# First attention: scores and searches in 64-row tiles, two heads side by side in two banks

## The reference, cut to what matters

```
qkv = x @ w_qkv.T + b_qkv
q, k, v = jnp.split(qkv, 3, axis=-1)            # 16 heads of 8 columns each
q, k = _apply_rope(q, cos, sin), _apply_rope(k, cos, sin)
scores = jnp.einsum('bhsd,bhtd->bhst', q, k) / jnp.sqrt(jnp.float32(hd))
scores = jnp.where(causal[None, None, :, :], scores, -jnp.inf)
attn = jax.nn.softmax(scores, axis=-1)
out = jnp.einsum('bhst,bhtd->bhsd', attn, v)
return out @ w_out.T + b_out
```

## Time and profile before

| | us |
|---|---|
| median of three runs | 3714.76 |
| the profiled execution, its own time | 3713.15 |
| its span (first to last instruction) | 3711.4 |
| PE busy | 3239.8 (87%) |
| DVE busy | 2656.9 (72%) |
| ACT busy | 2004.8 (54%) |
| POOL busy | 588.2 (16%) |
| first attention: first to last exponential (L952) | 345.0 to 972.0 |

### The profile page before, as it was taken

How to read it: one execution, slowest core, us unless ns; L and a number is a source line. 1 busy time by engine, 2 the same in 40 slices (tenths; PEclk the granted TensorE clock), 3 DMA queues, 4 the chain that set the end, 5 groups by cost and what they waited for, 6 DMA issues and landing times. The chain is left out here.

```text
span 3711.4 us, 44165 instructions
## 1 busy us (share of the span) xinstructions
PE 3239.8 (87%) x14402; PEld 1960.8 (53%) x14402; DVE 2656.9 (72%) x6064; ACT 2004.8 (54%) x3427; POOL 588.2 (16%) x484
## 2 busy tenths in 40 slices
PE   4999999999899998779988777778799998589998
PEld 3775343443377764236544333334477776357776
DVE  5566778777355587777766888886777777777776
ACT  2444656555444445444435655543377775157776
POOL 0000000000000000000002544430023332013332
PEclk9999999999999999889999889889999999789999
DMA  2000101010000131003331000002411110011111
GB/s 78 1 24 21 39 24 36 19 44 10 22 10 1 59 97 51 1 31 97 101 105 59 1 0 1 1 17 84 135 59 46 42 31 23 0 41 35 38 47 49
DMA packets 89647, 146.27 MB, mean 39 GB/s; under 512 B 13085, under 2 KB 25565, under 8 KB 89289
## 3 DMA queue, kind: packets, MB, share of 16 engines
q1 hardware_dynamic: 89416, 143.43, 12.5%
HBM read 134.02 MB, written 9.34 MB: 39 GB/s over the span
## 5 line engine op out<-in xcount | busy, mean ns | idle before, releaser
L358 POOL TENSOR_TENSOR norm_rstd<-norm_rstd,minus_half 128x4 f32<-128x4 f32 x144 | 174.3, 1211 | 2210.7 <-DVE norm_rstd L349 2208.2
L952 ACT ACTIVATE main_tiles<-banks 128x512 f32<-128x512 f32 (+3 forms) x768 | 356.9, 490 | 246.3 <-PE banks L940 166.3
L2189 ACT ACTIVATE main_tiles_r<-banks,feature_cols 128x512 fp32r<-128x512 f32 x512 | 353.2, 690 | 190.4 <-PE banks L228 168.5
L821 DVE TENSOR_REDUCE gate_scratch<-banks 128x1 f32<-128x512 f32 (+3 forms) x608 | 367.1, 655 | 122.4 <-PE banks L771 94.7
L2197 DVE TENSOR_TENSOR main_tiles_r<-main_tiles,main_tiles_r 128x512 fp32r<-128x512 f32 x512 | 383.4, 764 | 69.9 <-ACT main_tiles L2190 68.4
L226 PE MATMUL banks<-normed_pairs,moe_weights 128*128 128x512 f32 x800 | 409.2, 512 | 18.4 <-ACT main_tiles L2190 7.1
L2190 ACT ACTIVATE main_tiles<-banks,feature_cols 128x512 f32<-128x512 f32 x512 | 350.2, 684 | 0.0
L227 PE MATMUL banks<-normed_pairs,moe_weights 128*128 128x512 f32 x800 | 318.2, 398 | 0.0
L228 PE MATMUL banks<-normed_pairs,moe_weights 128*128 128x512 f32 x800 | 317.8, 397 | 0.0
L2234 POOL TENSOR_TENSOR normed<-normed,main_tiles 128x512 f32<-128x512 f32 x128 | 217.7, 1701 | 538.7 <-DVE main_tiles L2223 538.7
L226 PE MATMUL banks<-main_tiles_r,moe_weights 128*128 128x512 f32 x640 | 266.5, 416 | 28.3 <-DVE main_tiles_r L2197 26.4
(11 more groups left out here) (333 smaller groups left out, 6788.3 us busy)
## 6 DMA issues: line engine op xcount, KB each, us to landing
main_tiles<-gates_d SPq DMA_DIRECT2D x400, 256.0 KB, 3.3
weight_staging<-in_w SPq DMA_DIRECT2D x33, 256.0 KB, 3.7
parts_d<-bf_parts SPq DMA_DIRECT2D x48, 128.0 KB, 1.8
q_stacks<-parts_d SPq DMA_DIRECT2D x192, 32.0 KB
k_stacks<-parts_d SPq DMA_DIRECT2D x192, 32.0 KB
x_res<-in_x_t SPq DMA_DIRECT2D x8, 256.0 KB, 3.4
out_x<-x_res SPq DMA_DIRECT2D x8, 256.0 KB, 3.7
rope<-in_rope SPq DMA_DIRECT2D x1, 1024.0 KB
```

Of the source, the lines that this page charges most:

```text
L821: eng.tensor_reduce(o, bank[:, 0:per * (k1 - k0)].rearrange("p (n c) -> p n c", n=per), AX.X, ALU.max).then_inc(s.ring_free)
L952: eng.activation(weight_tile(e)[:, 0:C - q0], psum[:, 4 + e % 2, 0:C - q0], ACT.Exp, scale=HD ** -0.5).then_inc(s.at_exp)
L2189: eng.activation(pair_3(j)[0], psum[:, 2 + j % 2, :], ACT.Relu, bias=bias)
```

## The change

1. Each score or search matmul reads 64 rows only (`q_of`, `k_of`) and names a tile position, row 0 for an even head and row 64 for an odd one. Heads 2j and 2j+1 are issued one behind the other, to two different banks.
2. A mask is added by `add_mask`: since a 64-row tile sees only half of the identity's rows, there are two matmuls for a head, one from each half of the rows; the half that lies in the other 64 rows comes from a copy with the halves exchanged (`matb_swapped`). One of the two has 128 columns, the other 64. So four small matmuls stand for a pair of heads, where there were two.
3. Scores go through three banks (4, 5, 6), in pairs: a pair (e, e+1) waits for exponential e-2. The row sums use bank 7 alone (before 6 and 7), so that the first one of each half waits for the copy of the half before; it is planned 4.4 behind its head instead of 2.6.
4. The search has 40 items for a group (before 38), each of one parity of heads: for the first 128 queries two items of two heads (256 columns) in place of one of four heads. Items are issued in pairs; a pair (n, n+1) waits until item n-2 was reduced, and DVE starts on the pair when both are there.
5. Planned times: a group every 31.0, a head every 0.62, a search item every 0.7.
6. At the start four more DMAs (ahead of x), one more DVE copy, and the wait for constants counts nine loads (144).
7. The waits of the second feed-forward block and of the first scores follow the banks.

```diff
+    matb_swapped = at("const_mats_bf_swapped", [P, 3 * P], BF16)
...
-    raw = main[:, 21, :]
+    raw, raw_swapped = main[:, 21, :], main[:, 20, :]
+    def add_mask(eng, o, side, mask):
+        for half in range(2):
+            m = (matb if half == side else matb_swapped)[64 * side:64 * side + 64, :]
+            c0, c1 = (64 * half, TILE) if mask == 1 else (0, 64 * half + 64)
+            z = eng.matmul(o[:, c0:c1], m[:, 0:P], m[:, mask * P + c0:mask * P + c1], start=False, stop=half == 1,
+                           tile_position=(64 * side, 0))
+        return z
...
+        for half in range(2):
+            to, of = slice(64 * half, 64 * half + 64), slice(64 - 64 * half, 128 - 64 * half)
+            eng.dma_start(raw_swapped[to, 0:P], mats[of, 0:P]).then_inc(s.const_in, 16)
+            eng.dma_start(raw_swapped[to, P:3 * P], mats[of, MATS["mask_st"]:MATS["mask_st"] + 2 * P]).then_inc(s.const_in, 16)
...
-        eng.wait_ge(s.const_in, 80)
+        eng.wait_ge(s.const_in, 144)
...
+        eng.tensor_copy(matb_swapped[:, :], raw_swapped[:, 0:3 * P])
...
-    GROUP_US = 42.0
+    GROUP_US = 31.0
...
-    HEAD_US = 0.83
+    HEAD_US = 0.62
+    ITEM_US = 0.7
...
-    for i in range(4):
-        per = (4, 2, 1, 1)[i]
-        SEARCH += [(i, h0, per, 0, (i + 1) * TILE) for h0 in range(0, 4, per)]
-    for i in range(4, 8):
-        per = (4, 2, 1, 1)[i - 4]
-        SEARCH += [(i, h, 1, 0, C) for h in range(4)]
-        SEARCH += [(i, h0, per, C, (i + 1) * TILE) for h0 in range(0, 4, per)]
+    for i in range(8):
+        per, k0 = (2, 2, 1, 1)[i % 4], C * (i // 4)
+        if i >= 4:
+            SEARCH += [(i, side, side + 2 * j, 1, 0, C) for j in range(2) for side in range(2)]
+        SEARCH += [(i, side, side + 2 * j, per, k0, (i + 1) * TILE) for j in range(0, 2, per) for side in range(2)]
...
-        return qs_t[:, g % 3, h // 2, j0:j1]
+        return qs_t[64 * (h % 2):64 * (h % 2) + 64, g % 3, h // 2, j0:j1]
...
-        return ks_t[:, g % 3, h, j0:j1]
+        return ks_t[64 * (h % 2):64 * (h % 2) + 64, g % 3, h, j0:j1]
...
+                if m % 2:
+                    continue
...
+                if n >= 2:
+                    eng.wait_ge(s.ring_free, n - 1)
+                i, _, h0, per, k0, k1 = SEARCH[m]
+                diag, width = k1 == (i + 1) * TILE, k1 - k0
+                for j in range(per):
+                    for side in range(2):
+                        o, h = ring_bank(n + side)[:, j * width:(j + 1) * width], h0 + 2 * j + side
+                        z = eng.matmul(o, q_of(g, h, i * TILE, (i + 1) * TILE), k_of(g, h, k0, k1), start=True,
+                                       stop=not diag, tile_position=(64 * side, 0))
+                        if j == per - 1 and not diag:
+                            z.then_inc(s.ring_pe)
                     if diag:
-                        z = eng.matmul(bank[:, o0 + k1 - k0 - TILE:o0 + k1 - k0], ident_b, mask_st, start=False, stop=True)
+                        for side in range(2):
+                            z = add_mask(eng, ring_bank(n + side)[:, (j + 1) * width - TILE:(j + 1) * width], side, 1)
+                            if j == per - 1:
+                                z.then_inc(s.ring_pe)
+                continue
...
+            eng.wait_ge(s.ring_pe, n + 2 if kind == "search" and key[2] % 2 == 0 else n + 1)
...
+    def score_bank(e):
+        return psum[:, 4 + e % 3, :]
...
-                z = eng.matmul(psum[:, 4 + e % 2, 0:C - q0], k_of(g, h, i * TILE, (i + 1) * TILE),
-                               q_of(g, h, half * C + q0, half * C + C), start=True, stop=not diag)
+                for side in range(2):
+                    z = eng.matmul(score_bank(e + side)[:, 0:C - q0], k_of(g, h + side, i * TILE, (i + 1) * TILE),
+                                   q_of(g, h + side, half * C + q0, half * C + C), start=True, stop=not diag,
+                                   tile_position=(64 * side, 0))
+                    if not diag:
+                        z.then_inc(s.at_score)
                 if diag:
-                    z = eng.matmul(psum[:, 4 + e % 2, 0:TILE], ident_b, mask_ts, start=False, stop=True)
-                z.then_inc(s.at_score)
+                    for side in range(2):
+                        add_mask(eng, score_bank(e + side)[:, 0:TILE], side, 2).then_inc(s.at_score)
...
-                eng.wait_ge(s.at_score, e + 1)
+                eng.wait_ge(s.at_score, e + 2 - e % 2)
...
-                yield when + 2.6
+                yield when + (4.4 if i == 0 else 2.6)
                 a = 2 * g + half
                 if i == 0:
-                    if a >= 2:
-                        eng.wait_ge(s.at_acc, a - 1)
+                    if a:
+                        eng.wait_ge(s.at_acc, a)
...
-                    y = eng.matmul(psum[32 * k:32 * k + 32, 6 + half, q0:C], v_t[:, i, c9:c9 + 32],
+                    y = eng.matmul(psum[32 * k:32 * k + 32, 7, q0:C], v_t[:, i, c9:c9 + 32],
...
-                yield group_at[g] + HEAD_US * (16, 48)[half] + 4.4
+                yield group_at[g] + HEAD_US * (16, 48)[half] + 3.4
```

More of the change, by code:

```diff
@@ L581, in pe_ffn_hidden @@
                 if j == 64:
-                    eng.wait_ge(s.ffn_done, NC_)
+                    eng.wait_ge(s.at_exp, AT_EXPS)
+                if j == 65:
                     eng.wait_ge(s.at_acc, AT_ACCS)
@@ L687, in build @@
         begin = group_at[g] - 45.0
-        items += [(begin + 0.9 * n, ("search", g, n)) for n in range(len(SEARCH))]
-        items.append((begin + 0.9 * len(SEARCH) + 2.0, ("turn", g)))
+        items += [(begin + ITEM_US * n, ("search", g, n)) for n in range(len(SEARCH))]
+        items.append((begin + ITEM_US * len(SEARCH) + 2.0, ("turn", g)))
     items.sort()
+    pairs_of = {}
+    for when, key in items:
+        if key[0] == "search":
+            pairs_of.setdefault((key[1], key[2] // 2), when)
+    items.sort(key=lambda item: (pairs_of[item[1][1], item[1][2] // 2] if item[1][0] == "search" else item[0], item[1]))
     ring_no = {key: n for n, (_, key) in enumerate(items)}
@@ L761, in pe_ring @@
                 _, g, m = key
-                i, h0, per, k0, k1 = SEARCH[m]
+                if m % 2:
+                    continue
                 if m == 0:
                     eng.wait_ge(stack_in[g % 3], 416 * (g // 3 + 1))
[L765 to L769, removed]
-                    if diag:
-                        z = eng.matmul(bank[:, o0 + k1 - k0 - TILE:o0 + k1 - k0], ident_b, mask_st, start=False, stop=True)
+                if n >= 2:
[9 more added lines that the diff above has]
+                            z.then_inc(s.ring_pe)
+                    if diag:
+                        for side in range(2):
[3 more added lines that the diff above has]
+                continue
             elif kind == "turn":
@@ L816, in dve_ring @@
                 _, g, m = key
-                i, h0, per, k0, k1 = SEARCH[m]
+                i, side, h0, per, k0, k1 = SEARCH[m]
                 if m == 0 and g >= 2:
                     eng.wait_ge(s.shift_out, 16 * g)
-                o = best_of(g)[:, h0:h0 + per, i] if k0 == 0 else rest_of(g)[:, h0:h0 + per, i - 4]
+                heads_ = slice(h0, h0 + 2 * per - 1, 2)
+                o = best_of(g)[:, heads_, i] if k0 == 0 else rest_of(g)[:, heads_, i - 4]
                 eng.tensor_reduce(o, bank[:, 0:per * (k1 - k0)].rearrange("p (n c) -> p n c", n=per), AX.X,
@@ L903, in sp_shifts @@
             b, k = g // 4, g % 3
-            yield group_at[g] - 45.0 + 0.9 * len(SEARCH) + 4.5
+            yield group_at[g] - 45.0 + ITEM_US * len(SEARCH) + 4.5
             heads_ = shift_d[b, 4 * (g % 4):4 * (g % 4) + 4]
@@ L907, in sp_shifts @@
             eng.dma_start(heads_.rearrange("h i s -> (h i) s"), low_of(g)).then_inc(s.shift_out, 16)
-            yield group_at[g] - 45.0 + 0.9 * len(SEARCH) + 6.5
+            yield group_at[g] - 45.0 + ITEM_US * len(SEARCH) + 6.5
             eng.wait_ge(s.shift_out, 16 * (g + 1))
@@ L929, in pe_scores @@
             for e, when, half, i, h, q0, diag in weighed_heads(g):
+                if e % 2:
+                    continue
                 yield when
@@ L950, in act_exp @@
                     eng.wait_ge(s.at_pv, (e - 10) // 4 + 1)
-                eng.wait_ge(s.at_score, e + 1)
-                eng.activation(weight_tile(e)[:, 0:C - q0], psum[:, 4 + e % 2, 0:C - q0], ACT.Exp,
+                eng.wait_ge(s.at_score, e + 2 - e % 2)
+                eng.activation(weight_tile(e)[:, 0:C - q0], score_bank(e)[:, 0:C - q0], ACT.Exp,
                                scale=HD ** -0.5).then_inc(s.at_exp)
@@ L986, in dve_acc @@
                     eng.wait_ge(s.ffn_w3, NC_)
-                eng.tensor_copy(found(g % 4, half), psum[:, 6 + half, :]).then_inc(s.at_acc)
+                eng.tensor_copy(found(g % 4, half), psum[:, 7, :]).then_inc(s.at_acc)
     on_sp += [sp_attn_setup, sp_turned, sp_stacks, sp_shifts]
```

5 lines of the change are left out of this document (2 added, 3 removed).

## The result

| | before | after |
|---|---|---|
| median of three runs, us | 3714.76 | 3766.13 (3764.87 to 3768.70) |
| profiled span | 3711.4 | 3764.3 |
| first exponential at | 345.0 | 362.1 |
| groups 0 to 14 | 597.5 | 628.2 |
| group 15 | 29.5 | 33.0 |

The ratio is 1.0139, 95% interval 1.0116 to 1.0162. The forecast was 3618, the range 3578 to 3690. Of the 53 us of span, 51 lie in the stage that was changed: 17 before its first exponential, 31 in groups 0 to 14, 3.5 in group 15. Behind it are 1.7.

What follows compares the result with a forecast made beforehand. The attention was taken as bound by PE, with hand-overs on top and DVE next: 3713.15 - 104 (groups 0 to 14) - 4.5 (last group) + 10 (retiling) + 2.1 (start) = 3616.8, so 3618 as median; range 3578 to 3690.

Steps and rivals of the forecast that it cites:

- Pairs side by side: Score and search matmuls on PE: both tiles overlap, the second starting 0.03 us late; gain 6.3 us a group.
- lean group: Attention group with a whole search beside its scores and hardly anything else: forecast 27.1 us instead of 34.05.
- Masks: Mask matmuls on PE, 32 pairs of heads a group: four in 0.14 us instead of two in 0.11, +1.0 us.
- Hand-overs: Bank hand-overs between engines: 44 a group instead of 86, loss 4.0 us instead of 5.6, upper bound 9.
- rival B: Attention: pairs starve in hand-overs, needing two banks at once; lean group loses 9 us instead of 4; 3693 us; chance 0.13.
- rival D: Attention: the PE-ACT hand-over chain, not PE's own time, sets a group; time stays, 3710 us; chance 0.04.
- The planned times ... only set orders: Planned times 31.0, 0.62 and 0.7 in the attention: where the real pace is 33, orders stay; no cost given.
- The clock: PE's granted clock, read as 1.00 in every window; matmul times taken at 2.4 GHz, no term for a fall.
- One bank for the row sums: First row-sum block of each half waits for DVE's copy, covered by about 3 us: no cost taken.
- Retiling: Changes of PE tiling among scores and searches: 72 x 0.13 = 10 us lost, bounds 0 and 22.
- Start: Kernel start: four DMAs before x move the wait by 1.8 us, the added copy gives 0.3; +2.1 us.
- SP: Loads of a group's stacks: 26 issues take 8.9 us, search follows 17 us later; no cost, 6 us cover.

Runs made afterwards that it cites:

- e3: Changed kernel with its pairs, banks and planned times, but matmuls over all 128 rows and one mask matmul a head: 3832.3 us, ratio 1.0312.
- e7: Changed kernel with the planned times of before, search pairs through four ring banks, scores singly in two banks, row sums in bank 7: 3719.7 us, ratio 1.0013.
- e8: Changed kernel with the planned times of before, score pairs through three banks, row sums in bank 7, search items singly: 3718.6 us, ratio 1.0010.
- e1: Kernel before with only the planned times of the change (31.0, 0.62, 0.7): 3729.0 us, ratio 1.0040.
- e2: Changed kernel with the planned times of before (a group 42.0, a head 0.83, a search item 0.85): 3740.7 us, ratio 1.0068.
- e14: e7 with the planned times of the change (31.0, 0.62, 0.7): 3751.2 us, ratio 1.0097.
- e4: Changed kernel with the planned times of before and no pairs: 64-row matmuls singly, two score banks, two banks for row sums: 3735.4 us, ratio 1.0052.
- e6: e4 with each score matmul of group 15 issued twice in a row into the same bank: 3729.8 us, ratio 1.0045.
- e5: e4 with the search of group 0 and the scores of group 15 over all 128 rows: 3722.7 us, ratio 1.0020.
- e9: e7 with the search of group 0 and the scores of group 15 over all 128 rows: 3714.8 us, ratio 1.0002.
- e11: e7 with searches of groups 0, 3, 7, 11 and scores of groups 2, 6, 10, 15 over all 128 rows: 3703.4 us, ratio 0.9969.
- e13: Changed kernel with searches of groups 0, 3, 7, 11 and scores of groups 2, 6, 10, 15 over all 128 rows: 3780.9 us, ratio 1.0183.

## Why the prediction was wrong

- **Pairs side by side: right.** Of the two starts of a pair the second is 4 to 6 ns behind in the median, and the next pair starts 0.21 us later. The lag that I took at 0.03 is near 0. The Trainium skill, "TensorE: Matmul & The Clock Gate", Part 3, has some 4 ns there; the trace agrees with it, not with my value. In a lean group at full clock the tiles are worth 6.15 us (39.9 in e3, 33.75 with them), where I had 6.3 less 1.0 for masks; over the whole kernel e3 prices them at 66 us, against my 15 x 5.3 = 80 for groups 0 to 14.
- **Masks: right.** Four in 0.14 us (630.19 to 630.33), as taken.
- **Hand-overs: the step that failed.** "I take 4.0, nearer to the smaller number of hand-overs." With the lag near 0, PE is held 28.4 - 7.7 + 1.0 = 21.7 us in a lean group, which takes 33.75 at full clock: 12 us lost, three times the term and beyond its upper bound of 9. The lean group's miss, 6.65 us, is 100 of the 125 us by which groups 0 to 14 missed (628.2 against 503.5). Fewer hand-overs was not less waiting: while a pair waits at the head of PE's list for its second bank the other consumer starves (65.5 us of score loads behind DVE, a wait that the kernel before did not have). This looks like rival B's mechanism at a greater price, but the ring of three is not all of it: with four ring banks and single scores (e7), or search items singly (e8), a lean group still takes 32.4. How the 12 us divide between the banks, the order on PE's list and the chain between PE and ACT (rival D) stays open. B's own sum was 3693, above the 3690 at which I closed the range.
- **"The planned times ... only set orders. ... the orders stay": wrong.** Orders have a price: 14 us in the kernel before (e1), 25 in the changed one (e2), 31 in e7 (e14). Of it 12, 10 and 15 lie before the first exponential, where I had put nothing within 3, and the rest among the groups, where the ring's items changed neighbours.
- **The clock: missing.** I read 1.00 in every row and let it stand, although the change was to leave PE idler. It fell to 0.74 in the last group, which took 33.0 instead of the forecast 25.0. In e4 group 15 lost 10.8 us, and at least 6.5 of them are the clock (e6). How much of the changed kernel's 51 us it is stays open: 95 us at 1.2 GHz between 290 and 1023 bound it at 48. The lean group's 33.75, at a clock of 1.00, owes nothing to it.
- **One bank for the row sums: wrong.** "I take nothing." Two blocks now follow each other (1.71, x16), and ACT stands behind them 32 times, 48.8 us in all. What that costs in time was not measured by itself; e7 and e8 have the same single bank and beat the kernel before in groups 0 to 14.
- **Retiling: near in sum, by two errors.** 0.2 instead of 0.13 for a change back and forth, but 94 changes between 64 rows and full height in groups 0 to 14, not 144: some 9 us (94 x 0.1, an estimate), forecast 10. The 55 fewer around the row sums, which I had not counted, give part of it back.
- **Start: mis-sized.** +0.9, forecast +2.1, since the constants land sooner behind their last issue (4.94 to 7.53, where it was 2.60 to 6.87):

```profile
7.53 0.32 DVE L287 CAST router_w_r<-router_w 128x8 fp32r<-128x8 f32 x3 [6.44 <-DMA main_tiles<-in_mats]
...
9.13 1.12 PE L348 MATMUL banks<-const_mats,x_res 128*128 128x128 f32 x4 [9.13 <-DVE half_s_and_half_s_s L301]
```

- **SP: right.** No search waited for its stacks.

Of the 51 us, by medians: 20 are the tiles without pairs (e4, of them 11 in group 15, for the most part by the clock, and 6 before the first exponential), 5 more the pairs on top (e2), 25 the planned times. That is one path; along another, pairs and times with full rows cost 117 and the tiles give 66 back.

## What to carry to other kernels

Where engines hand over through two or three banks, count what one hand-over asks for, not how many there are: a pair wants its two banks at once, and everything behind it on the list waits too. Before taking freed PE time as saved, ask what else a group waits for: here a lean group gave back 0.3 to 1.7 us of some 7. A change that makes TensorE idler has to be priced at half clock in its quiet stretches; keeping those at full height paid here where matmuls went singly or with four ring banks (e5, e9, e11), and not in the changed kernel (e13). Planned times in a list scheduler are part of the change: try the new code with the old times first.

## What was not expected of the hardware

- Single 64-row matmuls let the granted clock fall where 128-row ones for the same exponentials kept it (0.58 against 1.00 over the last group), and issuing each of them twice brought it back and made the group shorter, 33.8 us instead of 40.3.
- A change between 64-row and 128-row tiling costs 0.1 us each way (0.32 between starts instead of 0.22).
- Single matmuls of two heads in neighbouring 64-row tiles overlap also without being issued as a pair, when they happen to stand next to each other. In e4 a score and a search matmul, each of which took 0.39 us, start together:

```profile
488.39 0.39 PE L959 MATMUL banks<-q_stacks,k_stacks 64*128 64x512 bf16 x1 [0.44 <-DVE gate_scratch L840]
488.39 0.39 PE L784 MATMUL banks<-k_stacks,q_stacks 64*128 64x512 bf16 x1
```
